# Where the bias additions of the first k quarter stand in VectorE's queue, in a pre-norm attention and mixture-of-experts kernel

## The chip, the cores and the metric

The kernel runs on the 8 cores of one Trainium2 chip. Each core computes one half of the sequence of one of four batches for the output, and needs the whole sequence of its batch for the attention sum. There is no communication between cores. The time is the device time in microseconds of the slowest core.

## The reference

```
x = x + attn(layernorm(x))
x = x + ffn(layernorm(x))

attn(X):  Q, K, V = split(X @ W_in.T + b_in);  Q, K = rope(Q), rope(K)   # first half of the features
          A = sum over s of (K / |K|) * V
          return (A * Q) @ W_out.T + b_out + X
ffn(x):   top 2 of 8 experts by x @ gate_w.T, softmax of the two logits as gates
          return sum over e of gate_e * (x @ expert_w[e] + expert_b[e])
```

x is 4 x 2048 x 2048. Every expert is computed for every token, and the gates (zero for six of eight) weight the results.

## The kernel before

S = 2048 tokens are 16 tiles of 128, taken in two passes of 8 tiles (`NTO`), the other half first (`sp_i` 1, then 0). D = 2048 is 16 chunks of 128 (`ND`) for the contraction and 4 quarters of 512 columns (`NQ`, `OCW`) for the output. Weights lie in float32 in HBM and are loaded by GpSimd's DMA queue as bf16 into two buffers `wbuf0` and `wbuf1`, one quarter at a time. Products go to two PSUM buffers `ps_m` of 128 x 512.

A pass goes like this:

1. `phase_ln1` (L389): layer norm of 8 tiles in 4 blocks of two. For each tile of the block SyncE loads x into `x_scr0` or `x_scr1` (L403), which are free once the tile before them has been normalised. VectorE takes the statistics (L268, L271); for both tiles together it makes variance plus epsilon and its reciprocal (L286, L289), ScalarE the square root (L295), VectorE the two scalars (L301, L303). Then for each tile VectorE writes the normalised tile in bf16 to `xln_scr` (L316), TensorE transposes it in 16 pieces into the PSUM buffers `ps_tr` (L336), VectorE copies the first half to `xlnT` (L374) and ScalarE the second (L382).
2. `after_tile`: when both tiles of a block are through, `_proj_qt` (L467) is called for each with quarter 0 of k. TensorE does 16 matmuls into one `ps_m` (L488) as soon as the weights, the tile of `xlnT` and the PSUM buffer are there. VectorE then adds the bias and writes to `k_sb` (L500); that frees the PSUM buffer.
3. `phase_proj` (L507): quarters 1 to 3 of k, then all four of v, 8 tiles each, through the same `_proj_qt`. Behind the quarters of v VectorE does rope and the norms of k.
4. `phase_pa` (L601): the sum A over the tokens of the pass.

After both passes come the projection of q, rope and transposes of q scaled by A, the output projection (L776), the second layer norm with the gate logits, and the eight experts (L1014), some 887 us of matmuls without a break.

There is no scheduler: each engine runs its instructions in the order in which the program text emits them, and an instruction that waits for a semaphore holds all that stand behind it on its engine. The five semaphores `sv` (VectorE), `sp` (TensorE), `sc` (ScalarE), `swp` and `sxp` (loads) count up; `self.free[name]` holds the semaphore and the value at which a buffer is free, as known when a wait is emitted, and `_wait_free` waits for that. A PSUM buffer is taken in turn by `psm_ctr`, so `_proj_qt` for the two tiles of a block takes the one and the other.

In the order of emission of the kernel before, VectorE's queue in step 1 and 2 holds for each block: statistics of both tiles, the chain, apply and copy of each tile, addition of each tile. TensorE's holds: transposes of both tiles, matmuls of both tiles.

Of the kernel before, what the change touches and what calls it, by code (L numbers as in the profile page):

```python
# [19 lines left out]
class Sem:  # L20
    __slots__ = ("h", "n")

    def __init__(self, h):
        self.h = h
        self.n = 0
# [7 lines left out]
class Builder:  # L33

    def __init__(self, S, D, E, OCW):
        assert D % 128 == 0 and S % 256 == 0 and D % OCW == 0
        self.S, self.D, self.E, self.OCW = S, D, E, OCW
        self.ND = D // 128
        self.NT = S // 128
        self.NTO = self.NT // 2  # L40
        self.NQ = D // OCW
        self.RH = D // 4
        self.nc = bass.Bass("TRN2", target_bir_lowering=False)
        self._uid = 0
        self.free = {}
        self.wdma_done = {}
        self.kv_evac = {}
        self.bias_stage_done = {}
        self.psm_ctr = 0
        self._ln2_pend = []  # L50

    def _nm(self, base):
        self._uid += 1
        return f"{base}_{self._uid}"
# [6 lines left out]
    def build(self):  # L61
        nc = self.nc
        S, D, E, OCW = self.S, self.D, self.E, self.OCW
# [69 lines left out]
        with contextlib.ExitStack() as ps_es, nc.Block() as blk:  # L133
            self._mk_psum(ps_es)
            ps_a = [ps_es.enter_context(
                nc.psum_tensor(self._nm("ps_a") + str(i), [1, OCW], F32))
                for i in range(NQ)]
            for sp_i in (1, 0):
                self._proj_bias(blk, "k")
                w_done_k0 = self._get_wdma(blk, "k", 0)  # L140
                self.phase_ln1(blk, sp_i, after_tile=lambda t: self._proj_qt(
                    blk, "k", 0, t, w_done_k0, first_t=(t == 0)))
                self.free["wbuf0"] = (self.sp, self.sp.n)
                self.phase_proj(blk, sp_i, "k", start_q=1)
                tpq = NTO // NQ

                def after_q(q, sp_i=sp_i, blk=blk, tpq=tpq):
                    if q == NQ - 1:
                        return
                    for t in range(q * tpq, (q + 1) * tpq):  # L150
                        self._rope_norm_k_tile(blk, sp_i, t)
                self.phase_proj(blk, sp_i, "v", after_quarter=after_q)
                self.phase_pa(blk, sp_i, ps_a, late=range((NQ - 1) * tpq, NTO))
            self._emit_wdma(blk, "q", 0)
            self.phase_a_roundtrip(blk)
# [308 lines left out]
            sbb.n += 16  # L464
        self.bias_done = sbb.n

    def _proj_qt(self, blk, which, q, t, w_done, first_t):  # L467
        NTO, OCW, ND = self.NTO, self.OCW, self.ND
        sc, sv, sp = self.sc, self.sv, self.sp
        dst = {"k": getattr(self, "k_sb", None),  # L470
               "v": getattr(self, "v_sb", None),
               "q": getattr(self, "q_sb", None)}[which]
        bias_done = self.bias_done
        self.psm_ctr += 1
        nm_ = len(self.ps_m)
        ps = self.ps_m[self.psm_ctr % nm_]
        pnm = f"psm{self.psm_ctr % nm_}"
        tile_rdy = self.tile_ready.get(t)

        @blk.tensor  # L480
        def _(te, q=q, t=t, ps=ps, w_done=w_done, pnm=pnm):
            te.wait_ge(self.swp[q % 2].h, w_done)
            if q == 0 and tile_rdy is not None:
                te.wait_ge(sv.h, tile_rdy[0])
                te.wait_ge(self.sc.h, tile_rdy[1])
            self._wait_free(te, pnm)
            for dc in range(ND):
                mm = te.matmul(  # L488
                    ps[:, :],
                    self.xlnT[:, dc, t * 128:(t + 1) * 128],  # L490
                    self.wbuf[q % 2][:, dc, :],
                    start=(dc == 0), stop=(dc == ND - 1))
            sp.inc(mm)
        mmc = sp.n

        @blk.vector
        def _(v, q=q, t=t, ps=ps, mmc=mmc, bias_done=bias_done):
            v.wait_ge(sp.h, mmc)
            v.wait_ge(self.sbb.h, bias_done)
            sv.inc(v.tensor_add(  # L500
                out=dst[:, t, q * OCW:(q + 1) * OCW],
                in0=ps[:, :],
                in1=self.bb_scr[:, q * OCW:(q + 1) * OCW]))
        self.free[pnm] = (sv, sv.n)
        self.kv_evac[(which, t)] = sv.n

    def phase_proj(self, blk, sp_i, which, after_quarter=None, start_q=0):  # L507
        NTO, NQ = self.NTO, self.NQ
        sp = self.sp
        if start_q == 0:  # L510
            self._proj_bias(blk, which)
        for q in range(start_q, NQ):
            w_done = self._get_wdma(blk, which, q)
            for t in range(NTO):
                self._proj_qt(blk, which, q, t, w_done, first_t=(t == 0))
            self.free[f"wbuf{q % 2}"] = (sp, sp.n)
            if after_quarter is not None:
                after_quarter(q)
        self.free["bb_scr"] = (self.sv, self.sv.n)
# [593 lines left out]
```

## Time and profile before

| what | value |
|---|---|
| time before, median of 3 runs | 2038.42 us (2038.17 to 2066.28) |
| the profiled execution's own time | 2037.19 us |
| its span on the slowest core (5) | 2035.6 us |
| spans of the eight cores | 2018.1 to 2035.6 us |
| mean granted TensorE clock of the cores | 0.906 to 0.914 |
| TensorE matmul busy | 1688.3 us (83%) |
| VectorE busy | 626.7 us (31%) |
| ScalarE busy | 87.0 us (4%) |
| projection matmuls (L488) | 2560, 582.2 us |
| expert matmuls (L1014) | 4096, 886.9 us |

The span runs from the first to the last instruction of the slowest core; the execution's own time is 1.6 us longer. Shares are means over stages with different limits. PE is TensorE, DVE VectorE, ACT ScalarE, POOL GpSimd, SP SyncE. A granted clock of 1.00 is 2.4 GHz, 0.50 is 1.2 GHz. Times in a timeline are microseconds from the span's start.

### The profile page before, as it was taken

The page shows a single profiled execution, that of the slowest core. Times are in us where ns is not written, and L with a number is a line of the kernel's source. Part 1 is how long each engine was busy: PE and PEld are TensorE (multiplying, and loading weights), DVE is VectorE, ACT ScalarE, POOL GpSimd, SP SyncE. Part 2 cuts the span into 40 slices and gives each one's busy share as a digit, 9 for nine tenths or more (in the row PEclk, how much of TensorE's full clock was granted, in tenths as well). Part 3 has the DMA queues.
Part 4 walks back from the last instruction along what each step waited for, and adds up shares of the span by engine and source line. Part 5 has one row for each costly group of instructions (what it writes and reads, how often), then busy time and mean ns, then how long its engine had stood idle before and what let it go on. Part 6 is the DMA issues. An engine that isn't in the chain of part 4 may idle for free.

```text
span 2035.6 us, 19634 instructions; the slowest of 8 cores (2018.1 to 2035.6 us)
## 1 busy us (share of the span) xinstructions
PE 1688.3 (83%) x7905; PEld 772.5 (38%) x7905; DVE 626.7 (31%) x1005; ACT 87.0 (4%) x134; POOL 69.8 (3%) x71
## 2 busy tenths in 40 slices
PE   2489589448958948946865999999999999999997
PEld 1244233224423413432333444444444444444442
DVE  2422053652114341265355222222222222222224
ACT  1210000121000000040000000000000000000000
POOL 1000000000000000000000000000000000000000
PEclk9789799778979978967976999999999999999997
DMA  9332653723365436328430554455554445554444
GB/s 172 98 42 42 93 84 72 134 93 42 42 93 88 68 47 99 42 70 173 83 47 2 83 76 68 72 75 83 83 83 66 71 71 83 83 83 71 69 68 165
DMA packets 132368, 161.80 MB, mean 79 GB/s; under 512 B 6577, under 2 KB 127409, under 8 KB 128185
## 3 DMA queue, kind: packets, MB, share of 16 engines
q0 software_dynamic: 118544, 120.66, 41.4%
q1 hardware_dynamic: 13738, 39.90, 6.1%
q8 instruction: 66, 1.08, 0.2%
q14 instruction: 20, 0.16, 0.0%
HBM read 272.79 MB, written 8.41 MB: 138 GB/s over the span
## 4 chain that ended last, share of the span: by engine, by line
PE 48%; DVE 3%; DMA 2%; issue 1%; DVEq 1%; ACT 0%; ACTq 0%; SPq 0%; POOLq 0%
PE ps_m L1014 44%; PE ps_m L776 3%; DMA x_scr<-x_all 1%; DVE st L268 1%; PE ps_tr L336 1%; DVE xln_scr L316 1%; DVE x L967 0%; DVE x L748 0%; DMA bb_scr<-biases 0%; DVE x2T L374 0%; DVE x L743 0%; DVEq L270 0%; PE ps_l L836 0%; DVEq L266 0%; ACT L295 0%
## 5 line engine op out<-in xcount | busy, mean ns | idle before, releaser
L1014 PE MATMUL ps_m<-wbuf,x2T 128*128 128x512 bf16 x4096 | 886.9, 380 | 0.2 <-issue 0.2
L488 PE MATMUL ps_m<-wbuf,xlnT 128*128 128x512 bf16 x2560 | 582.2, 391 | 100.0 <-DMA wbuf<-w_vT 45.2
L1014 PEld LDWEIGHTS ps_m<-wbuf,x2T 128*128 128x128 bf16 x4096 | 401.4, 98 | 485.3 <-issue 3.8
L488 PEld LDWEIGHTS ps_m<-wbuf,xlnT 128*128 128x128 bf16 x2560 | 256.3, 101 | 423.4 <-issue 141.1
L1027 DVE SCALAR_TENSOR_TENSOR x<-ps_m,gates,x 128x512 f32<-128x512 f32 x256 | 192.2, 751 | 695.3 <-PE ps_m L1014 695.3
L336 PE MATMUL ps_tr<-ident_bf,xln_scr 128*128 128x128 bf16 x384 | 45.2, 309 | 142.1 <-DVE xln_scr L316 142.1
L500 DVE TENSOR_TENSOR v_sb<-ps_m,bb_scr 128x512 bf16<-128x512 f32 x64 | 43.7, 690 | 208.0 <-PE ps_m L488 208.0
L500 DVE TENSOR_TENSOR k_sb<-ps_m,bb_scr 128x512 bf16<-128x512 f32 x64 | 44.3, 692 | 198.6 <-PE ps_m L488 198.6
L336 PEld LDWEIGHTS ps_tr<-ident_bf,xln_scr 128*128 128x128 bf16 x384 | 38.4, 142 | 149.9 <-issue 148.9
L776 PE MATMUL ps_m<-wbuf,qT 128*128 128x512 bf16 x384 | 86.4, 389 | 5.5 <-DVE x L789 5.5
L992 POOL DMA_DIRECT2D wbuf<-e_w x32 | 36.5, 1142 | 913.5 <-PE ps_m L1014 803.1
L776 PEld LDWEIGHTS ps_m<-wbuf,qT 128*128 128x128 bf16 x384 | 38.2, 100 | 53.1 <-issue 10.2
L500 DVE TENSOR_TENSOR q_sb<-ps_m,bb_scr 128x512 bf16<-128x512 f32 x32 | 22.0, 691 | 112.6 <-PE ps_m L488 85.0
L776 PE MATMUL ps_m<-x2T,qT 128*128 128x512 bf16 x128 | 33.4, 428 | 15.0 <-DVE x L789 11.0
L633 PE MATMUL ps_a<-v_sb,rn_bf 128*1 128x512 bf16 x64 | 19.4, 439 | 31.8 <-DVE v_sb L619 30.5
L268 DVE BATCH_NORM_STATS2 st<-x_scr 128x6 f32<-128x512 f32 x64 | 39.6, 681 | 15.7 <-DMA x_scr<-x_all 14.2
L336 PE MATMUL ps_tr<-ident_bf,q_sb 128*128 128x128 bf16 x128 | 14.7, 306 | 28.0 <-DVE q_sb L554 28.0
L567 DVE SCALAR_TENSOR_TENSOR tmp<-k_sb 128x2048 bf16<-128x2048 bf16 x16 | 36.7, 2292 | 2.5 <-DVE k_sb L554 2.5
L789 DVE SCALAR_TENSOR_TENSOR x<-ps_m,x 128x512 f32<-128x512 f32 x32 | 21.6, 680 | 46.5 <-PE ps_m L776 45.8
L587 ACT ACT_TABLE_LOAD x4 | 5.1, 1283 | 518.9 <-DVE tmp L567 518.9
L776 PEld LDWEIGHTS ps_m<-x2T,qT 128*128 128x128 bf16 x128 | 13.5, 107 | 34.6 <-issue 23.1
L295 ACT ACT_TABLE_LOAD x10 | 12.8, 1283 | 284.6 <-DVE st L289 284.6
(77 smaller groups left out, 387.7 us busy)
## 6 DMA issues: line engine op xcount, KB each, us to landing
wbuf<-e_w POOLq DMA_DIRECT2D x32, 2048.0 KB, 16.6
x_scr<-x_all SPq DMA_DIRECT2D x24, 1024.0 KB, 7.5
wbuf<-w_kT POOLq DMA_DIRECT2D x8, 2048.0 KB, 19.6
wbuf<-w_vT POOLq DMA_DIRECT2D x8, 2048.0 KB, 20.4
wbuf<-w_qT POOLq DMA_DIRECT2D x4, 2048.0 KB, 19.0
y<-x SPq DMA_DIRECT2D x8, 1024.0 KB, 6.3
wbuf<-w_oT POOLq DMA_DIRECT2D x3, 2048.0 KB, 27.0
bb_scr<-biases POOLq DMA_DIRECT2D x6, 512.0 KB, 7.3
```

Of the source, the lines that this page charges most:

```text
L268: v.bn_stats(out=sbuf[:, si, 6 * c:6 * c + 6], in_=x_in[:, c * cw:(c + 1) * cw])
L316: sv.inc(v.tensor_scalar(out=out_bf, in0=x_in, scalar1=sbuf[:, si, 28:29], scalar2=sbuf[:, si, 29:30], op0=ALU.mult, op1=ALU.add))
L336: tr = t.transpose(ps[:, (dc - lo) * 128:(dc - lo + 1) * 128], src_of(dc), self.ident_bf[:, :])
L488: mm = te.matmul(ps[:, :], self.xlnT[:, dc, t * 128:(t + 1) * 128], self.wbuf[q % 2][:, dc, :], start=(dc == 0), stop=(dc == ND - 1))
L500: sv.inc(v.tensor_add(out=dst[:, t, q * OCW:(q + 1) * OCW], in0=ps[:, :], in1=self.bb_scr[:, q * OCW:(q + 1) * OCW]))
L567: sv.inc(v.scalar_tensor_tensor(out=self.tmp8.rearrange("p a b -> p (a b)"), in0=self.k_sb[:, t, :], scalar=1.0, in1=self.k_sb[:, t, :], o ...
L633: mm = te.matmul(ps_a[qi][:, :], self.rn_bf[:, t:t + 1], self.v_sb[:, t, qi * OCW:(qi + 1) * OCW], start=is_first, stop=is_last)
L776: mm = te.matmul(ps[:, :], self.qT[:, dc, t * 128:(t + 1) * 128], rhs_of(dc), start=(dc == 0), stop=(dc == ND - 1))
L789: sv.inc(v.scalar_tensor_tensor(out=self.x1[:, t, q * OCW:(q + 1) * OCW], in0=ps[:, :], scalar=1.0, in1=self.x1[:, t, q * OCW:(q + 1) * OC ...
L992: g.dma_start(out=self.wbuf[si % 2][:, :, :], in_=self.e_w.rearrange("e (dc p) o -> e p dc o", p=128) [e_i, :, :, q * OCW:(q + 1) * OCW]). ...
L1014: mm = te.matmul(ps[:, :], self.x2T[:, dc, t * 128:(t + 1) * 128], self.wbuf[si % 2][:, dc, :], start=(dc == 0), stop=(dc == ND - 1))
L1027: sv.inc(v.scalar_tensor_tensor(out=self.x1[:, t, q * OCW:(q + 1) * OCW], in0=ps[:, :], scalar=self.gates[:, t, e_i:e_i + 1], in1=self.x1[ ...
```

## The change

The bias additions of quarter 0 of k are no longer emitted with the matmuls of their tile. `_proj_qt` gets a parameter `defer_evac`, with which it puts the addition on a list, `_pq_pend`; `_proj_flush` emits what is on it. The hook that `phase_ln1` calls after a block empties the list before it emits the block's matmuls, so that the additions of block i are emitted after the layer norm of block i+1; after the last block the list is emptied once more. Nothing else is deferred: quarters 1 to 3 and v and q go as before.

```diff
-                self.phase_ln1(blk, sp_i, after_tile=lambda t: self._proj_qt(
-                    blk, "k", 0, t, w_done_k0, first_t=(t == 0)))
+
+                def k0_hook(t, blk=blk, w_done_k0=w_done_k0):
+                    if t % 2 == 0:
+                        self._proj_flush()
+                    self._proj_qt(blk, "k", 0, t, w_done_k0,
+                                  first_t=(t == 0), defer_evac=True)
+                self.phase_ln1(blk, sp_i, after_tile=k0_hook)
+                self._proj_flush()
                 self.free["wbuf0"] = (self.sp, self.sp.n)
...
-    def _proj_qt(self, blk, which, q, t, w_done, first_t):
+    def _proj_qt(self, blk, which, q, t, w_done, first_t, defer_evac=False):
...
         mmc = sp.n
+        if defer_evac:
+            self._pq_pend.append((blk, which, q, t, ps, pnm, mmc))
+        else:
+            self._proj_evac(blk, which, q, t, ps, pnm, mmc)
+
+    def _proj_evac(self, blk, which, q, t, ps, pnm, mmc):
+        OCW = self.OCW
+        sv, sp = self.sv, self.sp
...
+        bias_done = self.bias_done
 
         @blk.vector
         def _(v, q=q, t=t, ps=ps, mmc=mmc, bias_done=bias_done):
...
         self.free[pnm] = (sv, sv.n)
         self.kv_evac[(which, t)] = sv.n
+
+    def _proj_flush(self):
+        pend, self._pq_pend = self._pq_pend, []
+        for (blk, which, q, t, ps, pnm, mmc) in pend:
+            self._proj_evac(blk, which, q, t, ps, pnm, mmc)
```

The lines of the kernel after are 7 further down in the layer norm (L268 becomes L275, L316 L323, L336 L343, L374 L381), the matmul L488 becomes L495, and the addition L500 becomes L519.

VectorE, kernel before, from the last copy of block 0 in pass 1 (`ps_tr_10` and `ps_m_41`, `ps_m_30` are PSUM buffers, `st1` the statistics):

```order
L374 COPY xlnT<-ps_tr_10 128x8x128
L496 UNCONDITIONAL_BRANCH
L500 TENSOR_TENSOR k_sb<-ps_m_41,bb_scr 128x512
L496 UNCONDITIONAL_BRANCH
L500 TENSOR_TENSOR k_sb<-ps_m_30,bb_scr 128x512
L409 UNCONDITIONAL_BRANCH
L264 UNCONDITIONAL_BRANCH
L268 BN_STATS st1<-x_scr0 128x6 x4
L271 BN_AGGR st1<-st1 128x2
```

VectorE, kernel after, the same place:

```order
L381 COPY xlnT<-ps_tr_10 128x8x128
L416 UNCONDITIONAL_BRANCH
L271 UNCONDITIONAL_BRANCH
L275 BN_STATS st1<-x_scr0 128x6 x4
L278 BN_AGGR st1<-st1 128x2
```

Both additions, which wait for the matmuls of block 0, have left the place between the copy and the statistics of block 1.

VectorE, kernel after, from the last copy of block 1 in pass 1:

```order
L323 TENSOR_SCALAR xln_scr1<-x_scr1,st1 128x2048
L378 UNCONDITIONAL_BRANCH
L381 COPY xlnT<-ps_tr_10 128x8x128
L515 UNCONDITIONAL_BRANCH
L519 TENSOR_TENSOR k_sb<-ps_m_41,bb_scr 128x512
L515 UNCONDITIONAL_BRANCH
L519 TENSOR_TENSOR k_sb<-ps_m_30,bb_scr 128x512
L416 UNCONDITIONAL_BRANCH
L271 UNCONDITIONAL_BRANCH
L275 BN_STATS st1<-x_scr0 128x6 x4
```

The same two additions, of block 0, stand here behind the copies of block 1. The matmuls of block 1 on TensorE write the same two PSUM buffers and so wait for them. Behind the last copy of block 3 four additions follow one another, those of block 2 and of block 3, where there were two. The rows of TensorE, ScalarE, GpSimd and SyncE are the same in both kernels.

## Rows read from the trace of the kernel before

**Rows 1.** The page: span, and two groups by line (busy, mean, idle before).

```profile
span 2035.6 us, 19634 instructions; the slowest of 8 cores (2018.1 to 2035.6 us)
...
L488 PE MATMUL ps_m<-wbuf,xlnT 128*128 128x512 bf16 x2560 | 582.2, 391 | 100.0 <-DMA wbuf<-w_vT 45.2
...
L336 PE MATMUL ps_tr<-ident_bf,xln_scr 128*128 128x128 bf16 x384 | 45.2, 309 | 142.1 <-DVE xln_scr L316 142.1
```

**Rows 2.** Waits, 398 to 470 us: total, times, longest.

```profile
PE ps_tr L336 <- DVE xln_scr L316: 37.6, 6, 10.9
...
DVE k_sb L500 <- PE ps_m L488: 21.3, 6, 4.4
```

**Rows 3.** Timeline of VectorE, pass 2, blocks 0 and 1: start, length, instruction.

```profile
397.44 0.69 DVE L374 COPY xlnT<-ps_tr 128x1024 bf16<-128x1024 bf16 x1 [1.37 <-PE ps_tr L336]
...
405.85 0.69 DVE L500 TENSOR_TENSOR k_sb<-ps_m,bb_scr 128x512 bf16<-128x512 f32 x1 [2.76 <-PE ps_m L488]
406.63 2.47 DVE L268 BATCH_NORM_STATS2 st<-x_scr 128x6 f32<-128x512 f32 x4
...
409.52 2.47 DVE L268 BATCH_NORM_STATS2 st<-x_scr 128x6 f32<-128x512 f32 x4
...
414.96 1.35 DVE L316 TENSOR_SCALAR xln_scr<-x_scr,st 128x2048 bf16<-128x2048 f32 x1 [0.23 <-DVE st L303]
417.68 0.69 DVE L374 COPY xlnT<-ps_tr 128x1024 bf16<-128x1024 bf16 x1 [1.38 <-PE ps_tr L336]
...
421.19 0.69 DVE L374 COPY xlnT<-ps_tr 128x1024 bf16<-128x1024 bf16 x1 [1.37 <-PE ps_tr L336]
```

**Rows 4.** Timeline of TensorE, pass 2.

```profile
398.03 7.64 PE L488 MATMUL ps_m<-wbuf,xlnT 128*128 128x512 bf16 x32
...
416.56 1.87 PE L336 MATMUL ps_tr<-ident_bf,xln_scr 128*128 128x128 bf16 x16 [10.89 <-DVE xln_scr L316]
...
421.78 7.71 PE L488 MATMUL ps_m<-wbuf,xlnT 128*128 128x512 bf16 x32
...
469.46 50.71 PE L488 MATMUL ps_m<-wbuf,xlnT 128*128 128x512 bf16 x231
```

**Rows 5.** Timeline of VectorE, two additions that need not wait.

```profile
335.70 1.28 DVE L500 TENSOR_TENSOR v_sb<-ps_m,bb_scr 128x512 bf16<-128x512 f32 x2
```

**Rows 6.** x loads, issue to landing: issued at 28.0; 31.4; 60.3 to 88.2; 396.1.

```profile
DMA to landing us min/median/max: 10.0/10.0/10.0
...
DMA to landing us min/median/max: 9.8/9.8/9.8
...
DMA to landing us min/median/max: 5.7/5.9/6.8
...
DMA to landing us min/median/max: 5.7/5.7/5.7
```

**Rows 7.** Timeline of TensorE, pass 1: matmuls of blocks 0, 1 and 3.

```profile
40.36 8.94 PE L488 MATMUL ps_m<-wbuf,xlnT 128*128 128x512 bf16 x32 [6.83 <-DMA wbuf<-w_kT]
...
65.75 8.23 PE L488 MATMUL ps_m<-wbuf,xlnT 128*128 128x512 bf16 x32
...
114.21 36.17 PE L488 MATMUL ps_m<-wbuf,xlnT 128*128 128x512 bf16 x163
```

**Rows 8.** Windows: stretch, length, PE, PEld, DVE, ACT, POOL busy, PEclk, DMA, GB/s.

```profile
41.00:44.20 3.20, 3.20 (x9) 1.07 (x8) 0.00 (x0) 0.00 (x0) 0.00 (x0) 1.00 1.18 173
...
53.00:56.00 3.00, 0.00 (x0) 0.00 (x0) 2.55 (x5) 0.00 (x0) 0.00 (x0) 0.74 0.01 3
...
59.00:62.00 3.00, 1.47 (x15) 1.50 (x16) 1.62 (x2) 0.00 (x0) 0.00 (x0) 0.50 0.00 0
...
1120.00:2007.00 887.00, 886.47 (x4095) 401.40 (x4096) 191.87 (x257) 0.00 (x0) 34.25 (x30) 1.00 0.50 74
```

**Rows 9.** Load of w_k's third quarter; then TensorE at the first v quarter.

```profile
DMA to landing us min/median/max: 18.9/18.9/18.9
...
227.56 36.84 PE L488 MATMUL ps_m<-wbuf,xlnT 128*128 128x512 bf16 x160 [22.57 <-DMA wbuf<-w_vT]
```

More of the change, by code:

```diff
@@ L50, in __init__ @@
         self._ln2_pend = []
+        self._pq_pend = []
     def _nm(self, base):
@@ L494, in _proj_qt @@
         mmc = sp.n
+        if defer_evac:
[5 more added lines that the diff above has]
+        sv, sp = self.sv, self.sp
+        dst = {"k": getattr(self, "k_sb", None),
+               "v": getattr(self, "v_sb", None),
+               "q": getattr(self, "q_sb", None)}[which]
+        bias_done = self.bias_done
         @blk.vector
```

## The prediction

> **What bounds the kernel now.** I read the page first. The slowest core spans 2035.6 us and this execution took 2037.19 us, 1.2 us under the median of 2038.42; the sum below is made against the profiled execution and then moved up by 1.2 [rows 1]. The projection matmuls (L488) leave TensorE idle for 100.0 us, most of it for loads of v weights, which this change doesn't touch. The transposes (L336) leave 142.1 us idle, all of it put down to the normalised tile on VectorE (L316). So what matters is a part of that second figure: the stage in which layer norm and the first quarter of k are interleaved. It runs twice, pass 1 at about 8 to 121 us and pass 2 at about 383 to 477 us, four blocks of two tiles each.
>
> Next I read who waits for whom inside pass 2. TensorE waits 37.6 us for L316, and VectorE waits 21.3 us for L488 [rows 2]. Each engine waits for the other in turn. The timelines show why. I write N(i) for VectorE's normalisation of block i, M(i) for its 32 matmuls. VectorE ends N(0) with the copy at 397.44, then stands at the two bias additions until M(0) has delivered, the second at 405.85, and only at 406.63 begins the statistics of block 1; its second copy of block 1 starts at 421.19 [rows 3]. M(0) starts at 398.03 and is over 7.64 later, M(1) starts at 421.78 [rows 4]. The step is 23.75 us, about the sum of M (8 us) and N (15 us), though they use different engines.
>
> **The change part by part.** Counts of instructions and the rows of TensorE, ScalarE, GpSimd and SyncE stay as they are. On VectorE the two additions of block i go behind N(i+1), in three of four blocks of each pass; the last two additions stay where they were. No DMA is added; x loads follow their own release, so they start earlier.
>
> *A steady step.* From the first statistics of a block to the start of its last copy is 421.19 - 406.63 = 14.56 us [rows 3]. In the new order the copy (0.69) is followed by two additions that no longer wait, 1.28 us as a pair [rows 5], and 0.09 later by the statistics (405.85 + 0.69 to 406.63 shows that 0.09). The new step is 14.56 + 0.69 + 1.28 + 0.09 = 16.62 us, if VectorE alone sets it. The additions are not saved: they are paid at full price, what goes is the wait in front of them.
>
> *What is late next.* VectorE. TensorE needs 7.6 to 8.9 us for M and 5.22 us from a block's first transpose to its first matmul (416.56 to 421.78) and so is idle part of each step. The x load of the second tile is the near rival: it can start when that tile is normalised, 1.37 us before the last copy, and is wanted 2.06 + 2.89 us after the copy's start (409.52 - 406.63 = 2.89). That is a budget of 6.3 us, where it had about 14. Undisturbed loads in this stage took 5.7 to 6.8 us [rows 6], so one of them can be some 0.5 us late.
>
> *The added wait.* M(i+1) needs a PSUM buffer, and both are now held until the additions of block i, which stand behind the copies of block i+1. Its first matmul starts when the first addition is over, 0.69 + 0.69 + 0.02 = 1.4 us after the copy starts, not 421.78 - 421.19 = 0.59 us after it. Behind this waiting matmul on TensorE stand only M(i+1) and the next transposes, which VectorE wants 10 us later. The shift is 0.8 us, and once per pass, since it is the same in every block and VectorE's cycle doesn't contain it. The Trainium skill (Perfetto Trace Analysis, section Matmuls) speaks against such an order: independent matmul groups should rotate through PSUM banks so that draining one overlaps the matmuls of the next. Here no draining would overlap. By the rule the stage would lose; by the rows above it pays 0.8 us per pass and gains many times that, because the buffers' wait is not the longest.
>
> *Pass 2.* Block 0 has no additions before it, so the statistics of block 1 can start at 397.44 + 0.69 + 0.09 = 398.22; the second tile's x, issued at 396.1, lands 5.7 us later at 401.8 [rows 6] against 401.11 wanted: 0.7 lost. The last copy of block 1 starts at 398.22 + 14.56 + 0.7 = 413.48, that of block 3 two steps later at 446.72, and M(3) at 448.1 in place of 469.46 [rows 4]. Gain 21.3 us.
>
> *Pass 1.* Here M(0) waits for k weights until 40.36 and ends at 49.30 [rows 7]. N(0) is over well before. Block 1's x loads were issued at 28.0 and 31.4 and land 10.0 and 9.8 us later, the second at 41.2 [rows 6], so VectorE can have its first tile normalised at 41.2 + 5.44 + 1.35 = 48.0 (5.44 is 414.96 - 409.52). TensorE is then still in M(0); the transposes follow at 49.30. The first copy comes 417.68 - 416.56 = 1.12 us later [rows 3, 4], the second 421.19 - 417.68 = 3.51 us after it at 53.93, M(1) at 55.33 in place of 65.75. Gain 10.4. Two steps follow: before (114.21 - 65.75) / 2 = 24.23 each [rows 7], now 16.62, so 7.61 each. Gain of the pass 10.4 + 15.2 = 25.6 us.
>
> *Late loads.* The first x load of block 2 in pass 1 would start at 48.2, when the k weights still flow (the DMA share is down to 0.01 only in the window from 53 us, rows 8), and the slowest of the undisturbed ones took 6.8. Bounds 0 and 6 steps at (10.0 - 6.3) = 22 us; I take 1.0 us, near the rows of the same stretch.
>
> *The clock.* At 59 to 62 us, after TensorE had stood for ten, the granted clock is 0.50, which is 1.2 GHz, and the transposes run there; 16 of them take 1.87 us, 8 take 0.94. M(0) of pass 1 ended at 49.30, and the mean of 0.74 over 53 to 56 us puts its fall near 54.4 [rows 8]. In the new order M(i) ends 1.4 + 7.7 = 9.1 us after the copy of its block starts, and the next transposes start 16.62 - (421.19 - 416.56) = 12.0 after it: TensorE stands only 3 us and should often still find 2.4 GHz. At twice the clock 8 transposes would cost 0.47 us less, on VectorE's path, for up to 12 tiles: bounds 0 and 5.6 us. I take the first tile of each of six blocks with 0.4: 2.4 us. The last M of a pass runs into the next stage, so what it loses to 1.2 GHz counts in the end: such an M took 8.23 and 7.71 us [rows 7, 4] where 32 matmuls of 0.2165 (886.47 / 4095, rows 8) make 6.93; bounds 0 and 2.1, I take 0.9. The Trainium skill (TensorE: Matmul & The Clock Gate, section "Wait — 56ns, not 53.3ns?") gives 106.7 and 55.6 ns for a 128-column transpose at the two clocks, by which the first term would be an estimated 0.41 per tile; no row here shows a transpose at full clock.
>
> *After the stage.* Everything behind it waits for TensorE or for loads issued by its progress, so it moves up whole. The second k quarter's weights are long there, the third's load is issued when quarter 0 ends, takes 18.9 us [rows 9], and has 128 x 0.2165 = 27.7 us to land. The v stall of 22.57 us [rows 9] begins with the last k addition, and moves with it.
>
> *Sum.* 25.6 + 21.3 - 1.0 + 2.4 + 0.9 = 49.2 us. 2037.2 - 49.2 = 1988.0, and 1989.2 on the scale of the median.
>
> **The rivals.** *A, x loads become the bound.* If the second load of a block takes 8 to 10 us, as with other traffic [10.0 and 9.8, rows 6], each of the five steps without slack is 1.7 to 3.7 us longer: 8.5 to 18.5 us, the 1.0 for late loads is in that, and the two clock terms (3.3) are lost as well: 2000 to 2010. For it: the budget falls from 14 to 6.3 us. Against: the weights have landed by 53 us [rows 8], and in the rest of the stage hardly anything but x moves. A milder form, 1 us each, gives 1993.
>
> *B, the clock never helps.* TensorE's stretches of idling are shorter but its work is still broken into pieces. Then 3.3 us are lost: 1992.5.
>
> *C, it is given back later.* The loads of v, q and o weights and of x are all exposed somewhere; if the eight cores fall differently on the shared memory, the two v stalls (45.2 us, rows 1) could grow by a fifth, 9 us or more: 1998 to 2005. Against: all cores do the same and move together.
>
> *D, slower than before.* The place is the long k stretch behind the stage: if TensorE left the denser stage at 1.2 GHz and stayed there, each matmul would take twice 0.2165 us, as M(0) of pass 1 did at its start, with 9 matmuls touched in 3.2 us [rows 8]. From about 230 slow matmuls (49.2 / 0.2165) the gain is gone; half of the 768 in both passes would give 1989 + 83 = 2072. Nothing in the trace speaks for it: after longer idling TensorE was back at full rate within M, or M would have taken 13.9 us and not 7.6 to 8.9.
>
> **How the numbers follow.** Forecast 0.66, A 0.14, B 0.10, C 0.08, D 0.02. Two per cent, about what a measurement of this kernel can tell from no change, is 40.8 us, so the border is 1997.7. Faster: the forecast, B but for 0.01, half of A: 0.82. Within 2%: 0.16. Slower: 0.02. The range goes down to 1983, where the whole clock term comes and no load is late, and up to 2003, into A and C.
>
> **What would show it.** In the profile after: the additions of blocks 0 to 2 pass without a wait on TensorE; M starts some 16 to 17 us apart, not 24; TensorE's wait for L316 in pass 2 falls from 37.6 us to 10 to 15; M(3) starts near 89 and near 422 (448.1 less pass 1's gain). Waits of the statistics for x beyond 1 us a block would speak for A, a granted clock of 0.50 at the first transposes for B, longer v stalls for C. It is wrong if the M steps are over 19 us, or if they are right and the end moves by less than 40 us.

## The result and the profile after

The changed kernel took 1991.35 us (median of 10 runs), the kernel before 2038.3 us beside it. The ratio is 0.9772, with a 95% interval of 0.9761 to 0.9784, which is 46.5 us less (46.9 by the two medians). In some executions the cores of one die run at a lower granted clock and the time is longer; the medians include these, the ratios and every range of runs given below leave them out. The spans of the eight cores in the profiled execution are 1971.8 to 1989.7 us, the slowest is now core 0. A second measurement (the run "after again" below) gave 0.9776 (0.9762 to 0.9789).

The page of the kernel after, against [rows 1]:

```profile
span 1989.7 us, 19486 instructions; the slowest of 8 cores (1971.8 to 1989.7 us)
...
L495 PE MATMUL ps_m<-wbuf,xlnT 128*128 128x512 bf16 x2505 | 586.0, 395 | 104.7 <-DMA wbuf<-w_vT 44.7
...
L343 PE MATMUL ps_tr<-ident_bf,xln_scr 128*128 128x128 bf16 x384 | 40.8, 290 | 95.4 <-DVE xln_scr L323 95.4
...
L275 DVE BATCH_NORM_STATS2 st<-x_scr 128x6 f32<-128x512 f32 x64 | 39.6, 681 | 25.0 <-DMA x_scr<-x_all 24.3
```

TensorE's idle time before the transposes fell from 142.1 to 95.4 us. The difference, 46.7 us, is about the gain, though the two pages show different cores (5 before, 0 after). The idle time before the projection matmuls rose from 100.0 to 104.7, and the statistics now wait for x. (55 records of L495 are missing from this trace.)

Who waits for whom between M(0) and M(3) of pass 2 on core 0 (total, times, longest), against [rows 2]:

```profile
PE ps_tr L343 <- DVE xln_scr L323: 12.7, 6, 2.5
...
PE ps_m L495 <- DVE k_sb L519: 3.2, 3, 1.1
...
DVE st L275 <- DMA x_scr<-x_all: 0.2, 1, 0.2
```

TensorE's wait for the normalised tile is 12.7 us where it was 37.6, and the row of VectorE waiting for the matmuls (21.3 us, the additions) is gone. The second row is new: the matmuls wait for their PSUM buffer. Its 1.1 us at a time hold a missing first record (M shows 31 matmuls on this core); where all 32 are there it is 0.69. VectorE's timeline of pass 2 on core 0, from the second copy of block 1, against [rows 3]:

```profile
392.10 0.69 DVE L381 COPY xlnT<-ps_tr 128x1024 bf16<-128x1024 bf16 x1 [1.37 <-PE ps_tr L343]
392.70 1.28 DVE L519 TENSOR_TENSOR k_sb<-ps_m,bb_scr 128x512 bf16<-128x512 f32 x2
394.07 2.47 DVE L275 BATCH_NORM_STATS2 st<-x_scr 128x6 f32<-128x512 f32 x4
...
396.96 2.47 DVE L275 BATCH_NORM_STATS2 st<-x_scr 128x6 f32<-128x512 f32 x4
...
404.72 0.69 DVE L381 COPY xlnT<-ps_tr 128x1024 bf16<-128x1024 bf16 x1 [0.97 <-PE ps_tr L343]
```

The copy, both additions as a pair of 1.28 us, and the statistics follow without a wait; 394.07 is 1.97 us after the copy's start. The copy of the first tile waits 0.97 us for its transposes, not 1.38. TensorE of pass 2, here on core 4 of the same execution, where no record of M is missing, against [rows 4]:

```profile
384.90 1.05 PE L343 MATMUL ps_tr<-ident_bf,xln_scr 128*128 128x128 bf16 x16 [2.58 <-DVE xln_scr L323]
388.00 1.86 PE L343 MATMUL ps_tr<-ident_bf,xln_scr 128*128 128x128 bf16 x16 [2.04 <-DVE xln_scr L323]
390.56 8.21 PE L495 MATMUL ps_m<-wbuf,xlnT 128*128 128x512 bf16 x32 [0.69 <-DVE k_sb L519]
401.04 1.05 PE L343 MATMUL ps_tr<-ident_bf,xln_scr 128*128 128x128 bf16 x16 [2.27 <-DVE xln_scr L323]
404.13 1.87 PE L343 MATMUL ps_tr<-ident_bf,xln_scr 128*128 128x128 bf16 x16 [2.04 <-DVE xln_scr L323]
406.69 8.67 PE L495 MATMUL ps_m<-wbuf,xlnT 128*128 128x512 bf16 x32 [0.69 <-DVE k_sb L519]
```

M starts 16.13 us apart (390.56 to 406.69) where it was 23.75; the step after it, to M(3) at 423.73, is 17.04 us. The transposes of the first tile take 1.05 us, those of the second 1.87. M itself is longer on this core than before, 8.2 to 8.7 us and not 7.7.

In pass 1 one step stands out. On core 0, VectorE at the statistics of block 2, then the transposes of that block, M(2) and M(3):

```profile
56.89 2.47 DVE L275 BATCH_NORM_STATS2 st<-x_scr 128x6 f32<-128x512 f32 x4 [1.82 <-DMA x_scr<-x_all]
...
61.46 2.47 DVE L275 BATCH_NORM_STATS2 st<-x_scr 128x6 f32<-128x512 f32 x4 [1.76 <-DMA x_scr<-x_all]
...
68.51 1.86 PE L343 MATMUL ps_tr<-ident_bf,xln_scr 128*128 128x128 bf16 x16 [5.13 <-DVE xln_scr L323]
...
74.94 8.65 PE L495 MATMUL ps_m<-wbuf,xlnT 128*128 128x512 bf16 x31 [1.02 <-DVE k_sb L519]
...
92.00 33.25 PE L495 MATMUL ps_m<-wbuf,xlnT 128*128 128x512 bf16 x143 [1.07 <-DVE k_sb L519]
```

Both tiles of block 2 waited for x, 3.6 us together, and TensorE stood 5.13 us before the transposes, which then took 1.86 us.

Since another core is now the slowest, differences are best read as means over the cores. This table is worked out from TensorE's timeline of all eight cores of each profiled execution; each entry is the mean length of a stretch in us. The last row moves by some us with the cores that are late in a run. Each column is one execution: those of "weights at block 1" and "keep warm" were the slowest of their runs (1995.1 and 1995.7 us), that of "gaps and block 2" the fastest (1981.9).

| stretch | before | after | keep wait | after again | in gaps | third x buffer | weights at block 1 | weights at block 2 | keep warm | gaps and block 2 | the same, warm |
|---|---|---|---|---|---|---|---|---|---|---|---|
| start to M(0), pass 1 | 38.8 | 37.7 | 38.6 | 37.4 | 37.9 | 43.1 | 38.3 | 38.8 | 37.3 | 39.0 | 37.9 |
| M(0) to M(1) | 25.7 | 16.5 | 25.7 | 16.6 | 15.4 | 14.2 | 15.1 | 14.9 | 17.0 | 13.5 | 14.9 |
| M(1) to M(2) | 24.6 | 19.5 | 24.9 | 19.5 | 19.8 | 16.2 | 16.5 | 16.5 | 19.7 | 17.1 | 16.3 |
| M(2) to M(3) | 24.2 | 16.8 | 24.3 | 16.8 | 16.9 | 16.0 | 21.3 | 17.2 | 16.7 | 16.9 | 17.3 |
| M(0) to M(3), pass 2 | 71.5 | 48.8 | 71.8 | 48.7 | 46.5 | 47.9 | 48.9 | 48.3 | 50.3 | 45.7 | 47.2 |
| start to the first expert matmul | 1113.8 | 1068.5 | 1117.6 | 1067.5 | 1065.9 | 1068.9 | 1071.5 | 1066.0 | 1069.4 | 1058.7 | 1057.9 |

Up to M(3) of pass 1 (113.3 before, 90.5 after) 22.8 us are gained, from M(0) to M(3) of pass 2 another 22.7; up to the first expert matmul it is 45.3. So what lies between and behind gives nothing back beyond 0.2 us. The whole spans of the eight cores fell by 45.3 us in the mean too, from 2026.9 to 1981.6.

### The profile page after: what moved, and what is told of

The parts are those of the page before. It is cut to its first block, busy times and chain, and to the rows that moved or that the text cites. A ratio compares the mean times of both kernels' runs of the same rounds, so it can differ in the third digit from the quotient of the medians.

```text
span 1989.7 us, 19486 instructions; the slowest of 8 cores (1971.8 to 1989.7 us)
## 1 busy us (share of the span) xinstructions
PE 1684.8 (85%) x7757; PEld 771.5 (39%) x7905; DVE 625.6 (31%) x1005; ACT 87.0 (4%) x134; POOL 69.9 (4%) x71
## 4 chain that ended last, share of the span: by engine, by line
PE 48%; DVE 3%; DMA 2%; issue 1%; DVEq 1%; ACT 0%; ACTq 0%; SPq 0%; POOLq 0%
PE ps_m L1038 44%; PE ps_m L800 3%; DMA x_scr<-x_all 1%; DVE st L275 1%; PE ps_tr L343 1%; DVE xln_scr L323 1%; DVE x L991 0%; DVE x L772 0%; DVE x L767 0%; DMA bb_scr<-biases 0%; DVE x2T L381 0%; DVEq L277 0%; PE ps_l L860 0%; DVEq L812 0%; DVEq L273 0%
## 5 line engine op out<-in xcount | busy, mean ns | idle before, releaser
L495 PE MATMUL ps_m<-wbuf,xlnT 128*128 128x512 bf16 x2505 | 586.0, 395 | 104.7 <-DMA wbuf<-w_vT 44.7
L495 PEld LDWEIGHTS ps_m<-wbuf,xlnT 128*128 128x128 bf16 x2560 | 258.0, 101 | 431.3 <-issue 154.6
L343 PE MATMUL ps_tr<-ident_bf,xln_scr 128*128 128x128 bf16 x384 | 40.8, 290 | 95.4 <-DVE xln_scr L323 95.4
L519 DVE TENSOR_TENSOR v_sb<-ps_m,bb_scr 128x512 bf16<-128x512 f32 x64 | 43.7, 690 | 210.4 <-PE ps_m L495 210.4
L519 DVE TENSOR_TENSOR k_sb<-ps_m,bb_scr 128x512 bf16<-128x512 f32 x64 | 43.6, 690 | 148.8 <-PE ps_m L495 148.8
L343 PEld LDWEIGHTS ps_tr<-ident_bf,xln_scr 128*128 128x128 bf16 x384 | 35.2, 133 | 102.2 <-issue 101.8
L519 DVE TENSOR_TENSOR q_sb<-ps_m,bb_scr 128x512 bf16<-128x512 f32 x32 | 22.1, 692 | 112.4 <-PE ps_m L495 85.4
L275 DVE BATCH_NORM_STATS2 st<-x_scr 128x6 f32<-128x512 f32 x64 | 39.6, 681 | 25.0 <-DMA x_scr<-x_all 24.3
L800 PE MATMUL ps_m<-x2T,qT 128*128 128x512 bf16 x125 | 33.7, 435 | 14.8 <-DVE x L813 10.3
L343 PE MATMUL ps_tr<-ident_bf,q_sb 128*128 128x128 bf16 x128 | 14.3, 300 | 28.2 <-DVE q_sb L578 28.2
L343 PEld LDWEIGHTS ps_tr<-ident_bf,q_sb 128*128 128x128 bf16 x128 | 12.4, 139 | 30.4 <-issue 30.4
```

Of the source, the lines that this page charges most:

```text
L275: v.bn_stats(out=sbuf[:, si, 6 * c:6 * c + 6], in_=x_in[:, c * cw:(c + 1) * cw])
L343: tr = t.transpose(ps[:, (dc - lo) * 128:(dc - lo + 1) * 128], src_of(dc), self.ident_bf[:, :])
L495: mm = te.matmul(ps[:, :], self.xlnT[:, dc, t * 128:(t + 1) * 128], self.wbuf[q % 2][:, dc, :], start=(dc == 0), stop=(dc == ND - 1))
L519: sv.inc(v.tensor_add(out=dst[:, t, q * OCW:(q + 1) * OCW], in0=ps[:, :], in1=self.bb_scr[:, q * OCW:(q + 1) * OCW]))
L800: mm = te.matmul(ps[:, :], self.qT[:, dc, t * 128:(t + 1) * 128], rhs_of(dc), start=(dc == 0), stop=(dc == ND - 1))
```

## The experiments

### Keep the wait

```diff
+                    if t % 2 == 1:
+                        m_done = self.sp.n
+
+                        @blk.vector
+                        def _(v, m_done=m_done):
+                            v.wait_ge(self.sp.h, m_done)
```

> The order of the changed kernel, with one wait put back: before it begins the statistics of the next block, VectorE waits until the matmuls of this block are over. Theory 1 (the gain is the overlap of N(i+1) with M(i), nothing else): the steps of M return to about 24 us and the time to 2034 to 2043 us, ratio to before 0.998 to 1.002; the late additions cost at most 0.8 us per pass. Rival (the gain comes from the place of the additions itself, back to back behind the copies, or from freeing anything earlier): the time stays below 2025 us.

Measured: 2038.84 us beside 2038.34, ratio 1.0004 (0.9993 to 1.0015). VectorE and TensorE in pass 2, slowest core (7), VectorE first:

```profile
422.23 1.28 DVE L525 TENSOR_TENSOR k_sb<-ps_m,bb_scr 128x512 bf16<-128x512 f32 x2
430.97 2.47 DVE L281 BATCH_NORM_STATS2 st<-x_scr 128x6 f32<-128x512 f32 x4 [7.46 <-PE ps_m L501]
```

```profile
399.11 7.74 PE L501 MATMUL ps_m<-wbuf,xlnT 128*128 128x512 bf16 x32
...
423.06 7.69 PE L501 MATMUL ps_m<-wbuf,xlnT 128*128 128x512 bf16 x32 [0.64 <-DVE k_sb L525]
...
446.96 7.68 PE L501 MATMUL ps_m<-wbuf,xlnT 128*128 128x512 bf16 x32 [0.63 <-DVE k_sb L525]
```

The additions still pass as a pair behind the copies, and the PSUM buffers are still late (0.64 us). With the wait of 7.46 us back in front of the statistics the step is 23.9 us and the whole gain is gone. The order as such is worth nothing; what it lets VectorE do during M is worth all of it. In the mean of the cores the first expert matmul starts 3.8 us later than before (1117.6 against 1113.8), though the time is the same, so such a mean can differ from the time of the slowest core by that much.

### One pass at a time

```diff
-                                  first_t=(t == 0), defer_evac=True)
+                                  first_t=(t == 0), defer_evac=(sp_i == 1))
```

and with `sp_i == 0` for pass 2 alone.

> Additions deferred in pass 1 only. Theory 1 (both passes gain by themselves, and the rest moves up whole): M(3) of pass 1 stands near 90.5 us (mean of the cores, 113.3 before), the steps of pass 2 stay at 23.8 us, and the time falls by 20 to 26 us, ratio 0.987 to 0.990. Rival (the loads behind the stage give part of it back, and the gain of the whole comes mostly from pass 2): under 15 us.

> Additions deferred in pass 2 only. Theory 1: the steps of pass 2 fall from 23.8 to 16.1 to 16.8 us, M(3) stands 22 to 23 us nearer to M(0), and the time falls by 20 to 25 us, ratio 0.988 to 0.990; with the run for pass 1 it sums to the 47 us of both. Rival (part of the whole gain is shared, so that each alone gives more or less): the two alone sum to under 38 or over 55 us.

Measured: pass 1 alone 2012.08 us, ratio 0.9878 (0.9854 to 0.9902), 24.9 us less by the ratio. Pass 2 alone 2018.11 us, 0.9903 (0.9881 to 0.9926), 19.8 us less. In the profiles the first expert matmul starts 22.8 and 23.0 us earlier (means of the cores, 1091.0 and 1090.8 against 1113.8). The two sum to 44.7 us in time and 45.8 up to the experts, where both together gave 46.5 and 45.3. So each pass gains by itself, as far as these intervals can tell. By the ratio pass 2 alone fell 0.2 us short of the 20 to 25 expected, by the medians it is 20.2; the interval holds both. Its profile is of its fastest run, 2012.34 us, while the other three lie at 2016.2 to 2018.3.

### Three ways to shorten VectorE's row, and the base beside them

The base:

> The changed kernel once more, as the base for the three runs beside it: ratio to before 0.976 to 0.979. In pass 1, VectorE waits for x loads of block 2 by 1 to 4 us in all, in pass 2 by under 1 us a step.

Measured: 1990.53 us, ratio 0.9776 (0.9762 to 0.9789). In front of the statistics of block 2 of pass 1 VectorE stands 1.5 to 4.1 us, 3.1 in the mean of the cores. In pass 2 it is under 1 us a step on six cores, as expected, but 1.6 and 1.9 us in the first step on cores 2 and 6.

*Additions in the gaps.* The list is no longer emptied by the hook but one addition at a time (`_proj_flush` gets a count for that), in the middle of the chain of block i+1 and between apply and copy of its first tile:

```diff
         sqrt_done = sc.n
+        if mid is not None:
+            mid()
...
+            ready = self._ln_chain(blk, self.st1, sp_i * NTO + t0, BL,
+                                   mid=lambda: self._proj_flush(1))
...
+                if t == t0:
+                    self._proj_flush(1)
```

> The two additions of block i stand inside N(i+1): the first where VectorE waits 1.68 us for ScalarE's square root, the second where it waits 0.97 to 1.37 us for the transposes of the first tile. Theory 1 (in the changed kernel VectorE's own row sets the step, and the additions are paid at 1.28 us plus 0.8 us once per pass for the late PSUM buffer): each of the six deferred pairs is 1.28 us cheaper and M starts 0.6 us after the copy, but the budget of the x load shrinks from 6.3 to 5.0 us against landings of 5.4 to 6.8, which gives back 0.5 to 1 us a step: 3 to 7 us less than the changed kernel. Rival (x loads already set the step): 0 to 2 us less, and the waits of the statistics for x grow by the same 1.3 us a step.

Measured: 1987.27 us, ratio 0.9759 (0.9745 to 0.9773), 3.3 us under the base by the medians; the four runs lie at 1986.4 to 1988.5, those of the base at 1990.3 to 1991.2. VectorE in pass 2, block 1 (core 4):

```profile
383.27 0.69 DVE L522 TENSOR_TENSOR k_sb<-ps_m,bb_scr 128x512 bf16<-128x512 f32 x1
384.95 0.16 DVE L308 SCALAR_TENSOR_TENSOR st<-st 128x2 f32<-128x2 f32 x1 [0.99 <-ACT st L300]
...
386.68 0.68 DVE L522 TENSOR_TENSOR k_sb<-ps_m,bb_scr 128x512 bf16<-128x512 f32 x1
387.74 0.69 DVE L381 COPY xlnT<-ps_tr 128x1024 bf16<-128x1024 bf16 x1 [0.37 <-PE ps_tr L343]
```

Each addition eats a wait that was there: the one for the square root is 0.99 us and not 1.68, the one for the transposes 0.37 and not 0.97. By the table pass 2 is 2.2 us shorter, pass 1 hardly: its step to block 2 stays near 19.5. So in pass 2 the additions were on VectorE's path. Three pairs at 1.28 us would save 3.8 us there; 2.2 came, and 0.9 of the difference is longer standing before the statistics, for x. In pass 1 x sets the pace: in front of the statistics of blocks 2 and 3 VectorE stands 4.4 and 2.0 us (means of the cores) where it was 3.1 and 0.8 in the base.

*A third x buffer.*

```diff
-                xs = self.x_scr[t % 2]
-                sxp = self.sxp[t % 2]
+                xs = self.x3[t % 3]
+                sxp = self.sxp[t % 3]
```

> A third x buffer, in the first two passes only, so that an x load of block i+1 can be issued a tile earlier. Theory 1 (x loads cost the changed kernel 3 to 4 us in pass 1 and under 1.5 us in pass 2): 3 to 6 us less than the changed kernel, and no wait for x in blocks 2 and 3. Rival (the first x loads and weights are bound by the transfer itself, and a third load in flight only slows the others): 0 to 1 us less, with longer landings.

Measured: 1990.38 us, 0.9775 (0.9761 to 0.9789): no difference. This is the rival's case. The steps to blocks 2 and 3 are 16.2 and 16.0 us, so the waits for x are gone, but TensorE starts later (core 5):

```profile
43.60 9.51 PE L497 MATMUL ps_m<-wbuf,xlnT 128*128 128x512 bf16 x32 [10.19 <-DMA wbuf<-w_kT]
```

The third load is issued at the start, beside the weights for M(0). These weights land 34.4 us after their issue (mean of the cores) and not 28.7. M(0) starts at 43.1 us (mean) and not 37.4, which takes back 5.7 of the 6.5 us by which the steps of pass 1 are shorter (a part of those 6.5 is no gain at all: M(0) to M(1) is short because M(0) is late). M(3) of pass 1 stands at 89.5 us where the base has 90.3.

*The second quarter's weights later.* GpSimd waits until block 1 is normalised:

```diff
+            if t0 == BL:
+                self.blk1_done = sv.n
...
+            if (which, q) == ("k", 1) and self.k1_after:
+                g.wait_ge(self.sv.h, self.k1_after)
```

> The load of k's second quarter in pass 1 is issued only after block 1 is normalised (near 54 us) and not at 10 us. It is wanted at about 97 us. Theory 1 (the two weight loads of 4 MB read each share the transfer with x in the first 50 us, and pass 1 starts late for it): weights of quarter 0 land near 30 us and not 37 to 40, the x loads of blocks 0 to 2 in 5 to 8 us and not 9 to 13, M(3) of pass 1 stands 5 to 12 us earlier, the time is 5 to 12 us less. Rival (each load is bound by its own packets, not by sharing): landings stay and the time is within 2 us of the changed kernel.

Measured: 1992.14 us, 0.9785 (0.977 to 0.98): no better than the base. Two things in the expectation were wrong. The first weights don't land sooner (M(0) at 38.3), so it isn't the second weight load that holds them up. And the step to block 2 did fall, from 19.5 to 16.5, but the next rose from 16.8 to 21.3: the delayed load, issued at 51 to 54 us, now runs beside the x loads of block 3. Those take 9.2 to 11.1 us on the eight cores, in the base 4.7 to 7.2; the x loads of block 2, now without it, take 4.8 to 6.3 us, in the base 7.4 to 9.6.

### The same load later still

```diff
-            if t0 == BL:
+            if t0 == 2 * BL:
```

> As the run that delayed k's second quarter, but its load is issued only after block 2 of pass 1 is normalised, near 70 us, when the x loads of block 3 are on the way. It then has some 27 us to land, and takes 19 to 20. Theory 1 (what block 2 lost in pass 1 is the x load sharing the transfer with that weight load, and delaying it to block 1 only moved the collision to block 3): all three steps of pass 1 are 16.1 to 17 us, M(3) stands near 87 us (mean), 3 to 4 us earlier than in the changed kernel, and the time is 2 to 4 us less, if the weights are not late for the second quarter. Rival (the x loads are slow in pass 1 for another reason, such as the other cores): the step to block 2 stays near 19.5 us.

Measured: 1987.95 us, ratio 0.9752 (0.9729 to 0.9775). The steps of pass 1 are 14.9, 16.5 and 17.2 us, M(3) stands at 87.4 us where the base had 90.3. The two x loads of block 2, issue to landing, in the changed kernel (core 0):

```profile
DMA to landing us min/median/max: 8.0/8.0/8.0
...
DMA to landing us min/median/max: 9.4/9.4/9.4
```

and with the weights later (core 2):

```profile
DMA to landing us min/median/max: 5.8/5.8/5.8
...
DMA to landing us min/median/max: 6.1/6.1/6.1
```

So what the step to block 2 lost was the x load sharing the transfer with the second quarter's weights. SyncE issues the one, GpSimd the other; the Trainium skill (DMA: Bandwidth & Descriptors, section "Issuing engines are not separate DMA queues") says that such transfers run on the same 16 engines and interleave, and the trace agrees: 8.0 and 9.4 us beside the weights, 5.8 and 6.1 without; over all eight cores 7.0 to 10.1 beside them and 4.8 to 6.5 without. The runs lie at 1984.0 to 1988.5 us, those of the base at 1990.3 to 1991.2. The gain is 2.6 us by the medians and 4.9 by the two ratios, whose intervals overlap, so its size is uncertain.

### Keep the clock up

```diff
+                @blk.tensor
+                def _(te):
+                    self._wait_free(te, "tr0")
+                    for _i in range(20):
+                        te.transpose(self.ps_tr[0][:, 0:128],
+                                     self.ident_bf[:, :], self.ident_bf[:, :])
```

> The changed kernel with 20 transposes of the identity, 128 x 128, added on TensorE before the transposes of each tile of the stage, into a PSUM buffer that the real ones overwrite (extra work, no effect on the result). In the changed kernel the first tile of a block finds 2.4 GHz (copy waits 0.97 us), the second 1.2 GHz (1.37 us). Theory 1 (the clock is lost in the idling between the two tiles): the second tile's copy waits 0.97 us too, six times 0.4 us, M(3) runs its 32 matmuls in 7 us and not 8 to 8.5, in all 3 to 5 us less. Rival (transposes don't hold the clock up, or they stand in the way of the real ones): within 1 us of the changed kernel, or more.

Measured: 1989.61 us, 0.9778 (0.9755 to 0.9801): no difference, the rival's case. TensorE in pass 2 (core 5; L433 are the added transposes), and VectorE's copy of the second tile:

```profile
402.63 1.38 PE L343 MATMUL ps_tr<-ident_bf,xln_scr 128*128 128x128 bf16 x16 [2.29 <-DVE xln_scr L323]
404.18 2.29 PE L433 MATMUL ps_tr<-ident_bf 128*128 128x128 bf16 x20 [0.18 <-DVE xlnT L381]
406.26 1.23 PE L343 MATMUL ps_tr<-ident_bf,xln_scr 128*128 128x128 bf16 x16
408.59 7.07 PE L502 MATMUL ps_m<-wbuf,xlnT 128*128 128x512 bf16 x32 [1.09 <-DVE k_sb L526]
```

```profile
407.15 0.69 DVE L381 COPY xlnT<-ps_tr 128x1024 bf16<-128x1024 bf16 x1 [1.68 <-PE ps_tr L343]
```

Half of theory 1 holds: M runs its 32 matmuls in 7.07 us. But the added transposes between the tiles here run at the slow clock, 2.29 us for 20, and end after the tile is ready; the real ones come behind them, and the copy waits 1.68 us and not 1.37. That isn't so everywhere: of the 48 blocks (blocks 1 to 3, two passes, eight cores) 16 show the copy waiting 0.96 to 1.10 us, as theory 1 has it, and 32 show 1.16 to 1.96. Up to M(3) VectorE doesn't wait for M, so the loss counts: 50.3 us from M(0) to M(3) in place of 48.7, and 0.4 us in pass 1. Behind M(3) nobody hides the matmuls, and there the full clock pays: from M(3) to the first v quarter it is 111.7 and 111.2 us in the two passes (means of the cores), in the base 112.7 and 111.9. So 2.0 us lost and 1.7 won nearly cancel.

### Together

The gaps and the late weights, then the added transposes as well. Both edits are those above.

> Additions in the gaps of the next block's chain, and the late load of k's second quarter, together. Theory 1 (the gaps gave little in pass 1 only because x loads set the step there): steps of 15 to 15.6 us in both passes, M(3) of pass 1 near 84 us, 8 us or so less than the changed kernel in all: 1981 to 1984 us. Rival (another load is late in its place): no better than the gaps alone, 1986 to 1988 us.

> The run before with the 20 added transposes per tile as well. Theory 1: a further 2 to 5 us less, 1978 to 1981 us, steps near 14.6 to 15 us. Rival (with shorter steps TensorE has no room for the added 1.1 us per tile, and they delay the matmuls or the transposes): 0 to 3 us more than without them.

Measured: 1985.05 us, ratio 0.9748 (0.9727 to 0.9769), and 1984.71 us, 0.9745 (0.9726 to 0.9764). The first is the best simple version: its runs lie at 1981.9 to 1987.8, those of the base at 1990.3 to 1991.2. Its median lies between what the theory (1981 to 1984) and the rival (1986 to 1988) expected. Against the base the intervals of the two ratios overlap a little, so the extra 5.5 us are likely, not clear. The steps of pass 1 were expected at 15 to 15.6 and are 13.5, 17.1 and 16.9: x is late again at a budget of 5.0 us, by 1.5 and 1.9 us in front of the statistics of blocks 2 and 3 (means). M(3) stands at 86.5, not 84. The added transposes change nothing measurable, where the theory had 2 to 5 us less.

## Why the prediction was right, point by point

The forecast of 1989.2 us (1983 to 2003) stands against 1991.35, the gain of 49.2 against 46.5. Every miss below that matters points the same way, so the sum isn't close because errors cancelled.

*The mutual wait.* Right, and shown by the run that keeps the wait: with it the ratio is 1.0004.

*The steady step, 16.62 us, less 0.4 for a faster first transpose.* Measured 16.13 in pass 2 (core 4, block 1 to 2; 17.04 for the next, with 0.98 us of waiting for x), and 48.8 us for three steps in the mean of the cores. The additions are paid at 1.28 us as forecast, and the run with the additions in the gaps shows that they were on the path.

*The added wait, 0.8 us once per pass.* TensorE's row shows 0.69 us in blocks 1 to 3. M starts 1.4 us after the second copy where it was 0.59, so 0.8 holds. It didn't add up over the blocks, as argued. The Trainium skill's rule (Perfetto Trace Analysis, section Matmuls) that the draining of one PSUM bank should overlap the matmuls of the next speaks against the order; here its price is this wait, and what it buys is that N(i+1) runs during M(i).

*Pass 1, first step.* Forecast M(1) 10.4 us earlier; the mean of the cores is 10.3 (64.5 to 54.2). That the two agree so well is partly luck: 1.1 us of the 10.3 is M(0), which started at 37.7 and not 38.8. The change doesn't move M(0), and it lies between 37.3 and 39.0 in all the runs but the one with the third x buffer. The step from M(0) to M(1) fell by 9.2 us.

*Late loads, 1.0 us.* This is the term of the sum that was too small. The step to block 2 is 19.5 us in the mean against the forecast's 16.2, 3.3 us for that one step, of which 0.4 is a slow first transpose. The prediction named the place (the first x load at 48.2, while the weights still flow) and took the undisturbed landings for its size; the second load, issued at 52, took 9.4 us too. It is rival A at one step of six, and the run with the weights at block 2 shows its cause. Elsewhere the waits for x are smaller: on core 0 one of 0.2 us in pass 2, but 1.35 us on core 5; in the mean of the cores 0.9 us in front of block 3 of pass 1 and 0.2 to 0.6 us a block in pass 2.

*The clock, first term: 0.4 us for the first tile of six blocks.* The copy waits 0.97 and not 1.38 us, 0.41 as forecast, in five of the six blocks of core 0. In block 2 of pass 1 TensorE had idled 5.13 us because x was late, and its transposes took 1.86 us; cores 1, 2, 3 and 5 show the same, while cores 6 and 7 ran them in 1.05 and 1.12 us after 2.78 and 4.08 us of idling. So 2.0 us in place of 2.4, on core 0 and in the mean. On core 0 the granted clock over the first tile's transposes in pass 2 is 1.00, over the second's 0.50 (columns as in [rows 8]):

```profile
388.00:389.00 1.00, 0.93 (x16) 0.76 (x14) 0.41 (x1) 0.00 (x0) 0.00 (x0) 1.00 0.00 0
390.90:392.90 2.00, 1.87 (x16) 1.63 (x16) 0.80 (x2) 0.43 (x1) 0.00 (x0) 0.50 0.98 397
```

*The clock, second term: 0.9 us gained in the last M.* This step failed, with the wrong sign. The clock falls between the two tiles' transposes, ahead of M. M started at 1.2 GHz before the change too, but now it stays there longer: the granted clock is 0.50 for the first 2 us of M(1) and the first 3 us of M(2) in pass 2 of core 4 (390.6 to 392.6, 406.7 to 409.7), where before it was 0.50 for 1 us on core 5 (421.8 to 422.8) and 0.86 in the next. So M takes 8.21 and 8.67 us where it was 7.71 [rows 4]. Why the clock comes back later was not tried. From M(3) to the first v quarter the mean of the cores is 112.8 and 112.3 us in the two passes, before it was 112.1 and 111.4: 1.6 us lost in place of 0.9 gained. About 1.3 us of it is in the 416 matmuls of the k quarters themselves, the rest in the wait for the v weights. The run with the added transposes shows that it is the clock: with it up, M took 7.07 us.

*Nothing given back later* (rival C). Right: it is 170.2 us from the first v quarter of pass 1 to M(0) of pass 2 against 170.5 before, and 533.9 from the first v quarter of pass 2 to the experts against 535.0.

Together: forecast 49.2, less 1.9 for late loads (2.9 where 1.0 stood), less 2.5 for the last M, less 0.4 for one slow transpose, makes 44.4, close to the 45.3 read from the means. The rest up to 46.5 lies within what changes from run to run. D did not occur: the 416 matmuls from M(3) on take 90.6 to 92.0 us on the cores with all records, and 90.1 at 0.2165 each, so there is no long stretch at 1.2 GHz.

## What to carry to other kernels

When two engines wait for each other in turn, look at the row of each for an instruction that waits for the other and stands in front of work that doesn't need it; moving it behind that work was worth about the shorter of the two stretches here (7.6 us a step, with M at 7.7), and a wait put back in its place is a clean test. Adding the bias late has a price of its own, because TensorE gets its PSUM buffer later: 0.69 us here. It is cheapest when the additions stand in gaps that VectorE has anyway. Then recompute the budget of every load whose buffer is released in that stage: here it shrank from 14 to about 6 us, and the first load to meet other traffic was late.

## What the runs showed of the hardware

- A weight load issued 20 to 40 us before it is wanted is not free: moved from 10 to about 53 us it made x late for block 3; moved to 70 us, the step to block 3 is 17.2, near the base's 16.8. A third x load issued beside the first weights made those 5.7 us later.
- Twenty transposes of 128 columns added after M and twenty more before the second tile's kept the granted clock at 1.00 up to the second tile only in a third of the blocks (16 of 48). On core 5 in pass 2 it was 0.50 while the second lot ran (404.2 to 406.2), but rose during the real transposes behind it (0.99 from 406.6 to 407.5), with nothing but transposes on TensorE in between, and M ran at full rate, 7.07 us. So here transposes alone brought the clock back. Without the added ones, the clock that falls ahead of M costs M 0.5 to 1 us against the kernel before (8.21 and 8.67 us on core 4, 7.71 before).
- The cores of a pair (0 and 1, 2 and 3, and so on) end 10 to 15 us apart in the profile after (3 to 13 before), and which is the later changes from run to run: cores 0 and 1 end at 1989.7 and 1976.8 after, at 1977.3 and 1988.7 in the second run of the same kernel. In the profile after, core 0 waits 44.7 us for v weights and core 1 39.8. The time is that of the later one, so a gain in one core's trace is not the gain in time: core 5 alone fell from 2035.6 to 1977.4 us. Why the cores of a pair differ wasn't tried.
